# Moving the last two tiles' copies to SyncE, ScalarE's root and attention behind the gelu, and another cut between the last two sets

## The chip, the cores and the metric

One core of a Trainium2 chip runs the whole layer. The metric is the device time of that core in microseconds (us): the median of three runs was 2102.76 us (2102.34 to 2111.96). The execution that was profiled took 2104.69 us, of which the span of the trace is 2102.9 us.

The names of the engines in rows: PE is TensorE, DVE is VectorE, ACT is ScalarE, POOL is GpSimd, SP is SyncE. An engine name with a q behind it (SPq, ACTq, POOLq) is the part of the engine that issues DMAs and reads values into registers.

## The reference

6250 nodes with 256 values each, and 200,000 edges sorted by their destination. Cut to what matters:

```
xn  = layernorm(x)
gnn = relu(softmax-weighted sum over the edges of (xn @ W)[src] into dst, 4 heads, + bias)
mix = linear attention over all nodes (8 heads, kv = k^T v / N), then gelu(. @ w1 + b1) @ w2 + b2 + xn
x   = x + gnn + mix                                   # x1
z   = layernorm(layernorm(x)) * gamma + beta
logits = z @ Wr + br                                  # 8 experts, the best two of each node
y   = sum over the two of share_e * (gelu(z @ W1[e] + b1[e]) @ W2[e] + b2[e])
out = x1 + y
```

## The kernel before

The nodes lie in 49 tiles of 128 (tile 48 has 106). The kernel runs one long list of **steps** s = 0 to 210. Each engine walks through the same steps in its own order, written out in the code, and semaphores join them. There is no scheduler: what stands where is set by the tables that a planner at the top of the function fills (route_at, job_at, table_at, piece_at_step, final_at).

In steps 0 to 168 every step takes one group of 1024 edges (gather on GpSimd, products on VectorE, sums on TensorE). The sums come in from high destinations to low, so tiles 48 to 0 become complete one after the other. From step route_at[t] on tile t goes through its **route**: denominators (VectorE), attention = a division per head (ScalarE, L2209, one step later), sum and statistics (VectorE, L1833 to L1843), root (ScalarE, L2215, two steps later; this is the square root of the variance, and it and the gelu need different function tables), norm, transpose and logits (three later), choice of experts (four later), places (five later), sorting of the tile's rows by expert (six and seven later, L2503 on TensorE, L2245 on ScalarE), and then **hand-out**: the sorted tile goes to DRAM (keep_sorted, L1438), and eight copies, one for each expert, carry 128 rows each to that expert's region (L1452 on SyncE, L2236 on ScalarE). Each copy needs two numbers, where from and where to, that are read from memory into registers of the engine that issues it. Two copies make one piece (t, k), k = 0 to 3.

Every tile belongs to one of four **sets**: 48-24, 23-10, 9-5, 4-0. When a set is routed, a **table** on VectorE (L1921 and on) assigns its blocks of 128 rows to experts. From step 82 on each step also carries one **block** job. On TensorE this is the transposition of its input (turn_x, L2400), the second product of the block two steps older (L2466 and L2468, below called "down") and the first product of its own (L2428, "up"). ScalarE copies the turned input (L2166), copies the expert's weights (L2178, W_now) and applies the gelu (L2193). VectorE copies the result of the block three steps older out of PSUM (L1815, "the copy of the step"); a down of a step waits for the copy of the same step, since both use one bank, and a copy waits until the result before last has been stored. The stores go from SyncE (L1415) or, for blocks from step 169 on that are not in the last set, from ScalarE (L2249, four steps behind the block). The last block is at step 200.

From step 171 on, finished tiles are put together: x1 comes back from DRAM (SyncE, L1485, at final_at[t]), GpSimd gathers the two expert rows (L1599), VectorE adds (L1999 and L2002, "combine", at final_at[t] + 2), and SyncE writes the output (L1490). SyncE's own step is called c; in each c the block loads (L1402) come first, then keep_sorted, then the hand-out, then L1485 and L1490.

Steps 169 and on are called the tail. Tile 1 has route_at 169 and tile 0 has 170. Four tiles are **rushed** (RUSHED: 10, 5, 1, 0): SyncE makes pieces 0 and 1 at c = route_at + 9, and ScalarE pieces 2 and 3 at its step route_at + 10 (hand_out_rest). For tiles 1 and 0 these are c = 178 and 179 on SyncE, steps 179 and 180 on ScalarE.

Of the kernel before, what the change touches and what calls it, by code (L numbers as in the profile page):

```python
# [36 lines left out]
NEAR = 6  # L37
CUTS = (24, 10, 5)
CLOSED = (1, 2, 3)
# [16 lines left out]
def gps_layer(nc, x, xT, src_cols, dst_cols, W_turned, att_cols, inner_cols, src, dst, gnn_W, att_src, att_dst, gnn_bias, w_qkv, b_qkv, kln_g, kln_b, vln_g, vln_b,  # L56
# [5 lines left out]
    FULL = NT - 1  # L62
# [44 lines left out]
    NS = NG - COUNTED  # L107
# [12 lines left out]
    mix_at, route_at, table_at, final_at = {}, {}, [], {}  # L120
# [35 lines left out]
    HANDS = NE // BY_TWO  # L156
    RUSHED = tuple(t for t in SORTED if any(t == lo for _, lo in SETS[1:]) or route_at[max(t - 1, 0)] < route_at[t] + HANDS and t - 1 in (lo for _, lo in SETS[1:]))
    piece_at_step, waiting = {}, []
    for c in range(route_at[SORTED[0]] + 9, route_at[0] + 10):
        waiting += [(t, k) for t in SORTED if route_at[t] + 9 == c and t not in RUSHED for k in range(HANDS)]  # L160
        now = len(waiting) if any(route_at[t] + 9 == c for t in RUSHED) else 1 + c % 2 if len(waiting) > HANDS else 1
        piece_at_step[c] = waiting[:now] + [(t, k) for t in RUSHED if route_at[t] + 9 == c for k in range(HANDS // 2)]
        waiting = waiting[now:]
# [75 lines left out]
    with ExitStack() as ctx:  # L239
# [244 lines left out]
        def general_value(eng):  # L484
            return eng.value_load(general[0:1, 0:1], min_val=0, max_val=1)
# [608 lines left out]
        def loop_stage(ph):  # L1094
# [202 lines left out]
            def jobs_with(s):  # L1297
                return job_at[s] if s in job_at else None
# [853 lines left out]
            def on_scalar(act):  # L2152
# [137 lines left out]
                def part_weight(b):  # L2290
# [11 lines left out]
                    last.then_inc(part_ready, 1)  # L2302

                with act.If(general_value(act) == 0):
                    act.wait_ge(shifted_ready, 2)
# [7 lines left out]
                    for s in range(STEPS):  # L2313
                        for t in range(FULL, -1, -1):
                            if route_at[t] + 2 == s:
                                root(t)
                            if route_at[t] + 1 == s:
                                attention(t)
                        if 2 <= s < PAIRS + 2:
# [24 lines left out]
                        if jobs_with(s - 1):  # L2344
                            gelu(*jobs_with(s - 1))
                        for t in range(FULL, -1, -1):
                            if route_at[t] + 3 == s:
                                take_tile(t)
# [6 lines left out]
                        for t in RUSHED:  # L2355
                            if route_at[t] + 10 == s:
                                for k in range(HANDS // 2, HANDS):
                                    hand_out_rest(t, k)
# [1414 lines left out]
```

## Time and profile before

| | us |
|---|---|
| median of 3 runs | 2102.76 |
| profiled execution | 2104.69 |
| its span | 2102.9 |
| TensorE busy | 1761.4 (84%) |
| VectorE busy | 1595.5 (76%) |
| GpSimd busy | 1455.5 (69%) |
| ScalarE busy | 1213.1 (58%) |

These shares are means over parts that differ. Between 1700 and 1850 us TensorE has no idle time; in the tail, which begins at 1889 us, no engine is busy all the time. A row's idle time in brackets tells how long the engine stood still ahead of that instruction and what ended this. To find a step in the tail, count the ups back from the last: the up of step 200 starts at 2071.01, and each step has one.

### The profile page before, as it was taken

To read this page: it belongs to the slowest core of one execution; us is meant where nothing else is said; L and a number is where in the kernel's file an instruction comes from. 1 tells how busy PE (TensorE), PEld (TensorE's weight loads), DVE (VectorE), ACT (ScalarE), POOL (GpSimd) and SP (SyncE) were. 2 spreads that over 40 slices of the span, in tenths; PEclk is the share of its full clock that TensorE was granted. 3 is DMA by queue.
4 is the path that set the end of the run, shared out by engine and by line. 5 is a ranking of instruction groups with operands and counts; after the bars stand their busy time and mean duration, and the time that the engine had idled before them with its cause. 6 is when DMAs were issued, how large, how long until landed. Compare 5 with 4: busy or idle time off the path is not lost. (4 is left out here: it accounts for less than half of the span.)

```text
span 2102.9 us, 40583 instructions
## 1 busy us (share of the span) xinstructions
PE 1761.4 (84%) x10047; PEld 1429.2 (68%) x10048; DVE 1595.5 (76%) x3938; ACT 1213.1 (58%) x2310; POOL 1455.5 (69%) x1586
## 2 busy tenths in 40 slices
PE   8499999678677777767888898988998999998795
PEld 6367777556565556545767777766887888886584
DVE  7678888567677777779888888978986898884343
ACT  4433333235455555434877787867875798965452
POOL 3277777777777777777766777775777777763463
PEclk9799999888787878777999999998999999999898
DMA  9676665686666666666677777786678777856683
GB/s 334 153 192 173 174 172 157 195 276 182 174 179 184 176 181 180 172 166 163 188 199 200 216 213 212 210 248 174 188 202 243 203 214 206 216 151 204 193 253 115
DMA packets 289176, 411.77 MB, mean 196 GB/s; under 512 B 108856, under 2 KB 211520, under 8 KB 285227
## 3 DMA queue, kind: packets, MB, share of 16 engines
q0 software_dynamic: 74208, 206.08, 36.5%
q1 hardware_dynamic: 196968, 187.45, 30.2%
q10 hardware_dynamic: 17762, 15.56, 2.7%
q8 instruction: 90, 1.47, 0.3%
q14 instruction: 148, 1.20, 0.2%
HBM read 354.61 MB, written 90.98 MB: 212 GB/s over the span
## 5 line engine op out<-in xcount | busy, mean ns | idle before, releaser
L1577 POOL DMA_INDIRECT rows_g<-node_table,src_all x1347 | 1283.4, 953 | 474.9 <-issue 408.1
L2388 PE MATMUL psB<-rows_g,pick_e 128*128 128x260 f32 x2704 | 747.6, 438 | 143.4 <-issue 120.8
L2388 PEld LDWEIGHTS psB<-rows_g,pick_e 128*128 128x128 f32 x2704 | 582.8, 221 | 267.0 <-issue 161.3
L1752 DVE TENSOR_TENSOR rows_g<-rows_g,psD 128x2048 f32<-128x2048 f32 x169 | 384.7, 2276 | 0.0
L2160 ACT ACTIVATE pick_n<-local_row 128x1024 bf16<-128x1024 bf16 x169 | 178.6, 1057 | 173.7 <-PE psA L2377 165.2
L2428 PEld LDWEIGHTS psC<-xnT,W_now 128*128 128x128 f32 x1904 | 232.5, 193 | 11.3 <-ACT W_now L2178 5.0
L2428 PE MATMUL psC<-xnT,W_now 128*128 128x128 f32 x1904 | 234.4, 277 | 2.0 <-ACT W_now L2178 1.8
L1723 DVE TENSOR_TENSOR pick_e<-psD,slot_all 128x1024 f32<-128x1024 f32 x169 | 203.4, 1204 | 0.1
L2156 ACT ACTIVATE local_row<-local_row,minus_id 128x1024 bf16<-128x1024 bf16 x169 | 191.6, 1134 | 15.9 <-DVE both_f L2062 8.7
L1599 POOL DMA_INDIRECT rows_g<-set_dram,places x98 | 95.2, 972 | 112.2 <-issue 62.3
L1815 DVE COPY xn<-psD 128x256 f32<-128x256 f32 x119 | 50.1, 421 | 155.8 <-PE psD L2484 53.1
L2377 PE MATMUL psA<-window,pick_n 128*128 128x24 bf16 x1352 | 59.5, 174 | 102.2 <-DVE psD L1733 55.8
L2377 PEld LDWEIGHTS psA<-window,pick_n 128*128 128x128 bf16 x1352 | 54.9, 99 | 125.1 <-issue 124.1
L1741 DVE TENSOR_TENSOR p_both_e<-rows_g,psD 128x64 f32<-128x64 f32 x169 | 48.6, 288 | 114.8 <-DMA rows_g<-node_table,src_all 108.5
L2178 ACT ACTIVATE W_now<-W_f 128x1024 f32 x119 | 125.2, 1052 | 18.0 <-issue 16.7
L2468 PE MATMUL psD<-W_f,hidT_more 128*128 x480 | 124.2, 403 | 0.0
L2222 ACT ACTIVATE xdT<-psA 128x256 f32<-128x256 f32 (+1 forms) x49 | 18.8, 385 | 178.2 <-PE psA L2477 178.2
L2468 PE MATMUL psD<-W_f,hidT 128*128 x472 | 119.4, 397 | 0.0
L2468 PEld LDWEIGHTS psD<-W_f,hidT_more 128*128 128x128 f32 x480 | 89.1, 196 | 17.8 <-issue 0.7
L2166 ACT ACTIVATE xnT<-psA 128x256 f32<-128x256 f32 x119 | 44.3, 373 | 98.6 <-PE psA L2400 83.5
L2468 PEld LDWEIGHTS psD<-W_f,hidT 128*128 128x128 f32 x472 | 85.9, 192 | 16.7 <-issue 0.2
L2516 PE MATMUL psC<-W_f,xnT 128*128 128x512 f32 (+1 forms) x196 | 89.9, 602 | 2.5 <-DMA xnT<-in_xT_dram 2.5
(389 smaller groups left out, 2920.2 us busy)
## 6 DMA issues: line engine op xcount, KB each, us to landing
local_row<-local_dram SPq DMA_DIRECT2D x169, 256.0 KB, 4.1
sent_dram<-sorted_dram SPq DMA_DIRECT2D x176, 128.0 KB
rows_g<-node_table,src_all POOLq DMA_INDIRECT x1347
set_dram<-xn SPq DMA_DIRECT2D x104, 128.0 KB
xnT<-in_xT_dram SPq DMA_DIRECT2D x96, 128.0 KB
xin<-sent_dram SPq DMA_DIRECT2D x90, 128.0 KB
sent_dram<-zero_dram SPq DMA_DIRECT2D x24, 384.0 KB
acc<-node_table SPq DMA_DIRECT2D x49, 128.0 KB
```

What stands on the lines that cost most here:

```text
L1577: pool.indirect_dma_start(out=rows_g[:, r, j], out_offset=None, in_=node_table, in_offset=bass.IndirectOffsetOnAxis(ap=src_all[:, g, j:j + ...
L1599: pool.indirect_dma_start(out=final_home(f)[0][0:rows, c], out_offset=None, in_=set_dram[span_of[x]], in_offset=bass.IndirectOffsetOnAxis( ...
L1723: dve.tensor_tensor(pick_e[:, r], ids_here.unsqueeze(1).broadcast_to([P, EG, P]), slot_all[:, g].unsqueeze(2).broadcast_to([P, EG, P]), AL ...
L1752: dve.tensor_tensor(heads, heads, p_here.unsqueeze(3).broadcast_to([P, EG, HEADS, C]), ALU.mult).then_inc(ph_ready, 1)
L2156: act.activation(local_row[:, r], local_row[:, r], ACT.Abs, bias=minus_id[:]).then_inc(away_ready, 1)
L2160: act.activation(pick_n[:], local_row[:, r], ACT.Relu, bias=1.0, scale=-1.0).then_inc(pick_n_ready, 1)
L2178: act.activation(W1_now[:].rearrange("p k n -> p (k n)"), W1_f[:, bass.ds(experts[n], 1)].rearrange("p e k n -> p (e k n)"), ACT.Copy).the ...
L2377: last = pe.matmul(ps_pick[:, j * 6 * HEADS:(j + 1) * 6 * HEADS], pick_n[:, j * P:(j + 1) * P], window[:, w].rearrange("p k a -> p (k a)") ...
L2388: last = pe.matmul(ps_sum[s % 2][:, 0:AW], pick_e[:, s % SLOTS, j], rows_g[:, s % RING, j, 0:AW], start=(j == 0), stop=(j == EG - 1))
L2428: last = pe.matmul(inner_bank(n)[:, c * P:(c + 1) * P], W1_now[:, k, c * P:(c + 1) * P], xnT[:, u, k], start=(k == 0), stop=(k == KT - 1))
L2468: last = pe.matmul(ps_small[:, down_at], turned_rows(n, kind)[:, c], W2_f[:, bass.ds(e, 1), c], start=False, stop=(c == HK - 1))
L2516: last = pe.matmul((ps_up, ps_hT)[u][0:rows, :], xnT[:, u, k, 0:rows], wkv_s[:, k], start=(k == 0), stop=(k == KT - 1))
```

## The change

Three edits. CUTS moves the last cut from 5 to 3, so the last two sets are tiles 9-3 (21 blocks) and 2-0 (13 blocks), where they were 9-5 and 4-0 with 17 each. The sum of the blocks and the step of each job stay; the blocks of steps 184 to 187 now belong to the third set. The third set's table moves from step 142 to 156, the filling with zeros before its last tiles (eight DMAs of 384 KB) from c = 137 to c = 149, and the rushed tile of that set is 3 instead of 5. The last cut's table stays at step 176. Three tiles instead of five are put together behind the last block.

For tiles routed at step 169 or later (tiles 1 and 0) SyncE makes all four pieces and ScalarE none. And in steps after 169 ScalarE's root and attention stand behind the gelu, where they stood first in the step.

```
-CUTS = (24, 10, 5)
+CUTS = (24, 10, 3)
...
-        piece_at_step[c] = waiting[:now] + [(t, k) for t in RUSHED if route_at[t] + 9 == c for k in range(HANDS // 2)]
+        piece_at_step[c] = waiting[:now] + [(t, k) for t in RUSHED if route_at[t] + 9 == c for k in range(HANDS if route_at[t] >= NS else HANDS // 2)]
...
+                def roots_and_attention(s):
+                    for t in range(FULL, -1, -1):
+                        if route_at[t] + 2 == s:
+                            root(t)
+                        if route_at[t] + 1 == s:
+                            attention(t)
...
-                        for t in range(FULL, -1, -1):
-                            if route_at[t] + 2 == s:
-                                root(t)
-                            if route_at[t] + 1 == s:
-                                attention(t)
+                        if s <= NS:
+                            roots_and_attention(s)
...
                         if jobs_with(s - 1):
                             gelu(*jobs_with(s - 1))
+                        if s > NS:
+                            roots_and_attention(s)
...
-                            if route_at[t] + 10 == s:
+                            if route_at[t] + 10 == s and route_at[t] < NS:
                                 for k in range(HANDS // 2, HANDS):
                                     hand_out_rest(t, k)
```

HANDS is 4 and NS is 169.

SyncE at c = 178, as a piece of the difference (rows with + are new). L1384 and L1402 are the load of a block, L1438 stores the sorted tile 0, L1449 and L1450 read the numbers of one piece, and L1452 issues a copy:

```order
+L1384 TENSOR_LOAD acc
+L1384 ISA x2
+L1402 ISA
+L1402 DMA pick_e<-sent_dram 128x256
 L1438 DMA sorted_dram<-weff 128x2x256
+L1449 TENSOR_LOAD cuts
+L1449 ISA x4
+L1450 TENSOR_LOAD cuts
+L1450 ISA x4
+L1452 ISA
+L1452 DMA sent_dram<-sorted_dram 16x2048
```

From here tile 1's pieces stand four times in a row instead of twice, then the outputs (L1490) and the x1 loads (L1485) of c = 178, then tile 0's four pieces instead of two, then those of c = 179. The block loads of c = 177 to 180 come one by one; before, all four stood at c = 180.

ScalarE at step 179, a piece of the difference. L2234 and L2235 read the two numbers of a copy:

```order
 L2193 ACTIVATE hidT_more<-psC,acc 128x128
-L2234 TENSOR_LOAD cuts
-L2234 ISA x2
-L2235 TENSOR_LOAD cuts
-L2235 ISA x2
-L2236 ISA
-L2236 DMA sent_dram<-sorted_dram 16x2048
```

The six rows with - stand four times in step 179 and four times in step 180, and all are gone; the store L2249 follows the gelu at once.

ScalarE from the end of step 172 to the gelu of step 173, before. L2222 takes tile 1's transposed rows:

```order
L2193 ACTIVATE hidT<-psC,acc 128x128
L2222 ACTIVATE xdT<-psA 128x256
L2166 ACTIVATE xnT<-psA 128x256
L2176 TENSOR_LOAD blk_expert
L2176 ISA x2
L2178 ISA
L2178 ACTIVATE W_now<-W_f 128x1024
L2193 ISA
L2193 ACTIVATE hidT_more<-psC,acc 128x128
```

And the same stretch now, from tile 0's root on:

```order
L2215 ACT_TABLE_LOAD
L2215 ACTIVATE std_r<-mv_r,eps_sq 128x1
L2222 ACTIVATE xdT<-psA 128x256
L2166 ACTIVATE xnT<-psA 128x256
L2176 TENSOR_LOAD blk_expert
L2176 ISA x2
L2178 ISA
L2178 ACTIVATE W_now<-W_f 128x1024
L2193 ISA
L2193 ACT_TABLE_LOAD
L2193 ACTIVATE hidT_more<-psC,acc 128x128
```

Tile 0's root stood ahead of step 172's gelu and now stands behind it, so L2222 comes after the root, and the gelu of step 173 now loads its table again, where before it was the gelu of step 172 that did. The number of table loads is the same.

## Rows read from the trace of the kernel before

**Rows 1.** Busy time by stretch: start:end, length, busy of each engine, clock, DMA.
```profile
1965.00:1990.00 25.00, 13.23 (x76) 11.18 (x75) 4.89 (x14) 5.74 (x15) 7.68 (x9) 0.80 0.60 182
```

**Rows 2.** Waits of TensorE, 1903 to 2075 us: total, times, longest.
```profile
PE psD L2466 <- DVE xn L1815: 15.6, 8, 8.6
```

**Rows 3.** Timeline of SyncE's queue: start, length, operation, count.
```profile
1957.12 0.39 SPq L1438 DMA_DIRECT2D sorted_dram<-weff  x1
1960.13 5.23 SPq L1452 DMA_DIRECT2D sent_dram<-sorted_dram  x4
1966.58 0.55 SPq L1485 DMA_DIRECT2D rows_g<-x_dram  x1
1969.89 5.60 SPq L1452 DMA_DIRECT2D sent_dram<-sorted_dram  x4
...
1974.11 1.38 SPq L1452 DMA_DIRECT2D sent_dram<-sorted_dram  x2
...
1976.23 0.87 SPq L1485 DMA_DIRECT2D rows_g<-x_dram  x2
1984.85 3.75 SPq L1402 DMA_DIRECT2D pick_e<-sent_dram  x4
...
1989.67 0.39 SPq L1485 DMA_DIRECT2D rows_g<-x_dram  x1
```

**Rows 4.** Timeline of ScalarE, in the tail.
```profile
1903.36 1.07 ACT L2209 ACTIVATE acc<-acc,rden_f 128x64 f32<-128x64 f32 x4
...
1906.50 1.12 ACT L2193 ACTIVATE hidT<-psC,acc 128x128 f32<-128x128 f32 x4
...
1922.17 0.36 ACTq L2249 DMA_DIRECT2D set_dram<-xn  x1
...
1954.39 1.28 ACT L2193 ACT_TABLE_LOAD   x1
...
1955.78 0.33 ACTq L2249 DMA_DIRECT2D set_dram<-xn  x1
...
1965.64 7.10 ACTq L2236 DMA_DIRECT2D sent_dram<-sorted_dram  x4
```

**Rows 5.** Timeline of VectorE, in the tail.
```profile
1904.46 0.43 DVE L1833 TENSOR_TENSOR psD<-acc,gnn_bias_b 128x256 f32<-128x256 f32 x1 [1.15 <-ACT acc L2209]
...
1907.03 0.42 DVE L1815 COPY xn<-psD 128x256 f32<-128x256 f32 x1 [0.28 <-PE psD L2468]
...
1926.44 0.42 DVE L1815 COPY xn<-psD 128x256 f32<-128x256 f32 x1 [0.18 <-DMA set_dram<-xn]
...
1987.54 0.42 DVE L1815 COPY xn<-psD 128x256 f32<-128x256 f32 x1 [0.56 <-PE psD L2468]
...
1993.03 0.48 DVE L1999 SCALAR_TENSOR_TENSOR rows_g<-rows_g,share 128x256 f32<-128x256 f32 x1 [3.94 <-DMA rows_g<-x_dram]
...
2084.96 0.48 DVE L1999 SCALAR_TENSOR_TENSOR rows_g<-rows_g,share,acc 128x256 f32<-128x256 f32 x1 [6.59 <-DMA rows_g<-set_dram,places]
...
2094.97 0.49 DVE L1999 SCALAR_TENSOR_TENSOR rows_g<-rows_g,share,acc 128x256 f32<-128x256 f32 x1 [1.52 <-DMA rows_g<-set_dram,places]
```

**Rows 6.** Timeline of TensorE, in the tail; the first row is from step 147.
```profile
1690.42 2.05 PE L2428 MATMUL psC<-xnT,W_now 128*128 128x128 f32 x16 [1.26 <-ACT W_now L2178]
...
1909.13 1.99 PE L2468 MATMUL psD<-W_f,hidT 128*128 x8
...
1975.77 0.39 PE L2466 MATMUL psD<-acc 24*128 24x256 bf16 x1 [8.64 <-DVE xn L1815]
1976.09 3.78 PE L2468 MATMUL psD<-W_f,hidT_more 128*128 x8
...
1991.54 2.05 PE L2428 MATMUL psC<-xnT,W_now 128*128 128x128 f32 x16
...
2015.92 1.95 PE L2428 MATMUL psC<-xnT,W_now 128*128 128x128 f32 x16
...
2067.09 1.95 PE L2428 MATMUL psC<-xnT,W_now 128*128 128x128 f32 x16
```

## The prediction

> **What bounds the kernel now.** I read the engine shares first, then busy time by stretch, then the waits of TensorE in the tail, and last the timelines of the five engines there. Through the last part of the edge steps TensorE never stands still. The tail is different: in 1965 to 1990 us TensorE works 13.23 of 25 us at a mean granted clock of 0.80, VectorE 4.89, ScalarE 5.74 [rows 1]. Nobody is the bottleneck there, so an order or a queue is. In the tail TensorE waits 15.6 us for VectorE's copy (the down of a step needs the copy of the step), 8.6 of it in one piece [rows 2]. That piece ends at 1975.77, step 180 [rows 6]: ScalarE was issuing four hand-out copies for 7.10 us [rows 4], its store stood behind them, and VectorE's copy waited for that store. This is the stall that the change takes away.
>
> Two more facts of the tail matter. First, SyncE issues slowly: four copies take 5.23 us from the first to the last (tile 1) and 5.60 us (tile 0) [rows 3]. The two copies of a piece take 1.38, so reading the numbers between two pieces costs 5.23 - 2*1.38 = 2.5 to 5.60 - 2*1.38 = 2.8 us. A piece is 3.9 to 4.2 us of SyncE's time. Second, VectorE's combines wait for x1 loads that SyncE issues in the same list: the load of c = 180 was issued at 1989.67 [rows 3], and VectorE stood 3.94 us until it landed, at 1993.03 [rows 5], step 182. x1 loads of c serve VectorE's step c + 2. So before the change SyncE was already, for one step, what the tail waited for.
>
> **Part 1, the copies.** All times here are those of the profiled execution, before any shift by part 2. The sorted tile 0 is stored at 1957.12, and the first copy follows at 1960.13, behind the reading of its numbers [rows 3]. Four pieces instead of two for tile 1 add 2*3.9 = 7.8 us. The x1 load of c = 178 moves from 1966.58 to 1974.4 and its end to 1975.0. A block load now stands ahead of tile 0's pieces; four of them took 3.75 us from first to last with three number reads between, so one with its read is some 1.15 us. Tile 0's four pieces start at 1975.0 + 1.15 + 2.8 = 1978.9 and end 3*4.1 + 1.4 later, at 1992.6; before, they ended at 1969.89 + 5.60 = 1975.5. So the two x1 loads of c = 179 go from 1976.23 to about 1993.4 and end at 1994.2. Landing takes 3.4 us (1993.03 against 1989.67), so they are there at 1997.4, and VectorE needs 1 us for the last combine. Its copy of step 182, at 1987.54 before [rows 5], comes at 1998.4 at the earliest, and with it step 182's down.
>
> On the other side, what does the removal give? The copy of step 180 needs only ScalarE's store, which is issued some 7 us earlier. TensorE goes through step 181's up by about 1982 to 1984 and then stands until 1998.8: 15 us of new idle time. The 8.64 us of ScalarE's stall and the smaller one after it do go, but what is late next is SyncE's x1 load, 17 us later than it was, and it decides. After such an idle time the first down is slow: 3.78 us at 1976.09, after 8.64 us idle, against 1.99 at 1909.13 [rows 6]; with the up behind it I take 2.1 us. So step 182's up starts at 1998.8 + 0.3 + 3.6 = 2002.7 (1991.54 before), and ends 11.3 us later than before. This is the first term: **+11.3**. Its bounds: with pieces of 3.4 us instead of 3.9 to 4.1 (2.0 us for the reads), four more pieces are 13.6 instead of 16 us, and with no slow down the term is 11.3 - 2.4 - 2.1 = 6.8; with pieces of 4.4 and a landing of 5 us it is 14.5.
>
> A rule of the Trainium skill speaks for the change here: in DMA: Bandwidth & Descriptors, under "Issuing engines are not separate DMA queues", it says that issuing on several engines at once only saves the sequencers' issue time, "which is usually small relative to the DMA itself". By that rule the move costs SyncE nothing that counts. The rows say that here it is not small, since each copy is preceded by its reads (3.9 us a piece). [...]
>
> **Part 2, root and attention behind the gelu.** Tile 1's attention (step 170) comes behind the gelu that ends at 1906.50 + 1.12 = 1907.62 and so ends at 1908.7; VectorE waited for it until 1904.46 [rows 4, 5]. VectorE is in order: first sum, statistics and tile 0's denominators move by 4.3 us, and the copy of step 171 behind them goes from 1907.03 to 1911.4. The down of that step, at 1909.13, follows to about 1911.8: 2.7 us. The same happens with tile 0, and one thing more: the gelu of step 173 gets a table load that it did not have. A store on ScalarE's queue behind such a load goes out only when it is done, 1.39 us behind the load's start (1954.39, 1955.78), where without it the store at 1922.17 went out right behind the weights' copy [rows 4]. By my count that store goes to about 1926, since the turned inputs come 2 us later and the load adds 1.8. VectorE's copy at 1926.44 waits for just this store [rows 5]. Second term: **+3.8**. Bounds: -1 (the weights' copies and the gelu now come 0.6 us earlier, and this is all that counts) to +5. What follows is one chain up to the sorted tile 0 at 1957.12, so the term adds to the first. The gelu's side gains nothing, since TensorE waits for VectorE's copies and not for the gelu.
>
> The page ScalarE: Activation LUTs ("What ACT_TABLE_LOAD costs") gives 1.28 us for the load and 1.38 us of drain for every switch. The load's 1.28 is in the rows. The four switches stay four; a drain would make the term 1.4 larger.
>
> **Part 3, the last cut.** The blocks of steps 184 to 187 no longer hang on tiles 1 and 0. TensorE did not wait for their loads before, so this gains nothing by itself; it only makes it harmless that the last copy of tile 0 is issued at 1992 instead of 1982. But their stores change from SyncE to ScalarE, which issues them a step later. With ScalarE's stores, ups 182 to 187 took (2015.92 - 1991.54)/5 = 4.88 us a step; with SyncE's, ups 187 to 199 took (2067.09 - 2015.92)/12 = 4.26 [rows 6]. Four steps change sides: 4*0.62 = **+2.5** (0 to 3).
>
> At the end three tiles are gathered and combined instead of five. The first combines came at 2084.96 and 2094.97 for tiles one and five, 2.50 us apart [rows 5]: **-5.0** (-4.5 to -5.5), all on the path that ends the kernel. The combines of tiles 4 and 3 stand in the steps before, where VectorE is more than half idle.
>
> **Part 4, in the edge steps.** The third set's table, its zero filling and ScalarE's rushed copies move by 12 to 14 steps. The rushed copies of tile 5 cost TensorE 1.26 us, at step 147 [rows 6]; those of tile 3 will cost about as much. The table and the filling come into steps where TensorE has no slack and leave steps where it has some: I take **0**, with -3 and +3 as bounds.
>
> **Sum.** 11.3 + 3.8 + 2.5 - 5.0 + 0 = +12.6 on the profiled execution's 2104.69: 2117.3. The median of the runs is 1.93 lower, so 2115.4; I say 2115.
>
> **Rivals.**
> (a) The copies' issue is hidden, as the skill's rule would have it. Then steps 179 to 183 run at 4.88 us each; step 183's up, 5.0 behind that of 182, was at 1996.5, and step 179's, just ahead of the four copies, at about 1965.0, so 31.5 becomes 19.5: -12. With -5.0, +2.5 and part 2 at 0 to 3.8 this is -14.5 to -10.7, a median of 2088 to 2092: faster. For it speaks that ScalarE's two stalls are real; against it the x1 load behind the last copy, which has no way around. 12%.
> (b) The same mechanism as in my forecast, but part 2 is about 0 and the reads are at their cheap end: 8.9 + 0 + 2 - 5 = +6, a median of 2105 to 2111, no measurable change. For it: part 2 hangs on a chain that I count. 25%.
> (c) The change does nothing to the pace because the set boundary was what held the tail (the first load of the last set at 1984.85 waits for the last copy). The new boundary then gives four blocks of slack and the end is 5 us earlier, with part 1 gone: about 2100. I see no wait of TensorE for that load; 5%.
> (d) As my forecast, with the upper bounds of parts 1, 2 and 4, or a clock that stays low for longer after 15 us idle: +18 and more, above 2120. 13%.
> My forecast proper, 2111 to 2120, has 45%.
>
> **Chances.** A measurement of this kernel tells 0.5% (10.5 us) from no change. Slower by more: three quarters of the forecast (above 2113.3) and (d), 0.34 + 0.13, with a little of (b), 0.50. Faster by more: 0.12 of (a). The rest, 0.38, is within. The range is 2100 to 2123: it leaves out (a) and the far end of (d).
>
> **What would show it.** Right: no hand-out row of ScalarE after 1950; sixteen copies in SyncE's queue over some 33 us; VectorE's longest tail wait is at a combine, for x1, 10 us or more; TensorE's longest idle time is in step 182 and above 12 us, ended by VectorE's copy, with a slow down behind it; the store of step 173 later by 2 to 4 us against the end of the last sums; three combines at the end. Wrong: no idle time over 5 us in steps 181 to 183 (then the copies cost less than their rows say), or tile 0's sorted store at the same distance from the last sums (then part 2 is nothing), or edge steps that end at another time than 1889 by more than 3 us.

## The result and the profile after

| | before | after |
|---|---|---|
| median, us (lowest to highest, 7 runs each) | 2103.78 (2100.78 to 2111.96) | 2121.88 (2117.59 to 2123.41) |
| profiled execution | 2104.69 | 2123.41 |
| its span | 2102.9 | 2121.6 |

The ratio is 1.0075 (95% interval 1.0059 to 1.0091): slower by 0.75%, which is more than the 0.5% that a measurement tells from no change.

Five marks cut the tail into pieces that can be compared one by one: the ups of steps 169, 182, 187 and 200, and the store of the sorted tile 0 on SyncE. The lines above L2301 kept their numbers, those of TensorE's block work moved by 6 (L2428 is now L2434, L2466 is L2472, L2468 is L2474).

| piece of the span, us | before | after | difference | predicted |
|---|---|---|---|---|
| start to up of step 169 | 1902.7 | 1907.6 | +4.9 | 0 (-3 to 3) |
| to the store of sorted tile 0 | 54.4 | 58.5 | +4.1 | +3.8 |
| to up 182 | 34.4 | 44.5 | +10.1 | +11.3 |
| to up 187 | 24.4 | 26.1 | +1.7 | +2.5, up to 200 |
| to up 200 | 55.1 | 57.8 | +2.7 | in the line above |
| to the end | 31.9 | 27.0 | -4.9 | -5.0 |
| sum | 2102.9 | 2121.6 | +18.7 | +12.6 |

SyncE's queue after (start, length, line, operation, count) answers to [rows 3]:

```profile
1966.16 0.39 SPq L1438 DMA_DIRECT2D sorted_dram<-weff  x1
1969.11 13.45 SPq L1452 DMA_DIRECT2D sent_dram<-sorted_dram  x8
...
1983.81 0.42 SPq L1485 DMA_DIRECT2D rows_g<-x_dram  x1
...
1987.98 12.92 SPq L1452 DMA_DIRECT2D sent_dram<-sorted_dram  x8
...
2001.65 0.85 SPq L1485 DMA_DIRECT2D rows_g<-x_dram  x2
```

Sixteen copies stand between 1969.11 and 2000.90, with the one x1 load of c = 178 between the two groups of eight, and the two of c = 179 behind the second. The waits of VectorE and TensorE in 1885 to 2122 us (engine, line waited with, releaser: total, times, longest) answer to [rows 2]:

```profile
DVE rows_g L1999 <- DMA rows_g<-x_dram: 28.1, 3, 16.5
...
PE psD L2472 <- DVE xn L1815: 31.1, 11, 12.0
```

Before, the combines waited 7.2 us in all for x1. VectorE's timeline after, for [rows 5]; the number in brackets is the idle time ahead of a row:

```profile
1913.64 0.43 DVE L1833 TENSOR_TENSOR psD<-acc,gnn_bias_b 128x256 f32<-128x256 f32 x1 [5.40 <-ACT acc L2209]
...
1935.12 0.43 DVE L1815 COPY xn<-psD 128x256 f32<-128x256 f32 x1 [2.47 <-DMA set_dram<-xn]
...
1986.70 0.48 DVE L1999 SCALAR_TENSOR_TENSOR rows_g<-rows_g,share 128x256 f32<-128x256 f32 x1 [10.23 <-DMA rows_g<-x_dram]
...
2004.49 0.49 DVE L1999 SCALAR_TENSOR_TENSOR rows_g<-rows_g,share 128x256 f32<-128x256 f32 x1 [16.45 <-DMA rows_g<-x_dram]
...
2006.34 0.42 DVE L1815 COPY xn<-psD 128x256 f32<-128x256 f32 x1
...
2108.59 0.48 DVE L1999 SCALAR_TENSOR_TENSOR rows_g<-rows_g,share,acc 128x256 f32<-128x256 f32 x1 [5.70 <-DMA rows_g<-set_dram,places]
...
2113.58 0.48 DVE L1999 SCALAR_TENSOR_TENSOR rows_g<-rows_g,share,acc 128x256 f32<-128x256 f32 x1 [1.51 <-DMA rows_g<-set_dram,places]
```

And TensorE's, for [rows 6]:

```profile
1916.25 0.28 PE L2472 MATMUL psD<-acc 24*128 24x256 bf16 x1 [2.29 <-DVE xn L1815]
...
1988.19 0.39 PE L2472 MATMUL psD<-acc 24*128 24x256 bf16 x1 [7.37 <-DVE xn L1815]
1988.51 3.78 PE L2474 MATMUL psD<-W_f,hidT 128*128 x8
...
2006.91 0.39 PE L2472 MATMUL psD<-acc 24*128 24x256 bf16 x1 [11.97 <-DVE xn L1815]
2007.22 3.63 PE L2474 MATMUL psD<-W_f,hidT_more 128*128 x8
2010.69 1.95 PE L2434 MATMUL psC<-xnT,W_now 128*128 128x128 f32 x16
...
2094.62 1.95 PE L2434 MATMUL psC<-xnT,W_now 128*128 128x128 f32 x16
```

Read together: each group of eight copies holds up one x1 load, each late load holds up one combine, and behind each combine stands the copy that the down waits for. So 8.64 us of idle time [rows 6] became 7.37 + 11.97. The combines at the end are three: 2108.59 to 2113.58 is two times 2.50 us, where [rows 5] has four times.

Busy time by stretch (length, busy of TensorE, weight load, VectorE, ScalarE, GpSimd, granted clock, DMA share, GB/s) shows the hole beside the stretch of [rows 1], which is now the better one:

```profile
1983.00:2008.00 25.00, 7.83 (x30) 6.36 (x31) 4.37 (x13) 3.07 (x9) 3.18 (x4) 0.57 0.43 128
...
1965.00:1990.00 25.00, 16.40 (x105) 14.05 (x104) 5.92 (x15) 11.03 (x29) 8.92 (x11) 0.87 0.53 156
```

### The profile page after: what moved, and what is told of

Its sections match the earlier page's. It is cut to its first block and busy times, and to the rows that moved or that the text cites. A ratio compares the mean times of both kernels' runs of the same rounds, so it can differ in the third digit from the quotient of the medians.

```text
span 2121.6 us, 40575 instructions
## 1 busy us (share of the span) xinstructions
PE 1770.1 (83%) x10047; PEld 1437.4 (68%) x10048; DVE 1597.1 (75%) x3938; ACT 1213.6 (57%) x2310; POOL 1455.2 (69%) x1586
## 5 line engine op out<-in xcount | busy, mean ns | idle before, releaser
L1752 DVE TENSOR_TENSOR rows_g<-rows_g,psD 128x2048 f32<-128x2048 f32 x169 | 384.8, 2277 | 0.0
L2434 PEld LDWEIGHTS psC<-xnT,W_now 128*128 128x128 f32 x1904 | 234.8, 194 | 10.9 <-ACT W_now L2178 4.1
L2434 PE MATMUL psC<-xnT,W_now 128*128 128x128 f32 x1904 | 235.5, 277 | 2.7 <-ACT W_now L2178 2.6
L2383 PEld LDWEIGHTS psA<-window,pick_n 128*128 128x128 bf16 x1352 | 54.4, 99 | 115.8 <-issue 111.1
L2474 PE MATMUL psD<-W_f,hidT_more 128*128 x480 | 125.8, 407 | 0.0
L2474 PE MATMUL psD<-W_f,hidT 128*128 x472 | 122.5, 404 | 0.0
L2222 ACT ACTIVATE xdT<-psA 128x256 f32<-128x256 f32 (+1 forms) x49 | 18.9, 385 | 166.1 <-PE psA L2483 166.1
L2166 ACT ACTIVATE xnT<-psA 128x256 f32<-128x256 f32 x119 | 44.5, 374 | 115.4 <-PE psA L2406 115.4
L2474 PEld LDWEIGHTS psD<-W_f,hidT_more 128*128 128x128 f32 x480 | 90.1, 198 | 18.1 <-issue 0.4
L2474 PEld LDWEIGHTS psD<-W_f,hidT 128*128 128x128 f32 x472 | 87.9, 196 | 17.6 <-issue 0.4
```

The lines of the kernel that those rows point to most:

```text
L1752: dve.tensor_tensor(heads, heads, p_here.unsqueeze(3).broadcast_to([P, EG, HEADS, C]), ALU.mult).then_inc(ph_ready, 1)
L2383: last = pe.matmul(ps_pick[:, j * 6 * HEADS:(j + 1) * 6 * HEADS], pick_n[:, j * P:(j + 1) * P], window[:, w].rearrange("p k a -> p (k a)") ...
L2434: last = pe.matmul(inner_bank(n)[:, c * P:(c + 1) * P], W1_now[:, k, c * P:(c + 1) * P], xnT[:, u, k], start=(k == 0), stop=(k == KT - 1))
L2474: last = pe.matmul(ps_small[:, down_at], turned_rows(n, kind)[:, c], W2_f[:, bass.ds(e, 1), c], start=False, stop=(c == HK - 1))
```

## The experiments

Each was timed against the kernel before on the same chip. "Tail" is the distance from the up of step 169 to the end of the span, 200.2 us before and 214.0 after. It is the better measure of a change to the tail, because the start of step 169's up differs between profiled executions of like edge steps by some us. The columns behind the median are three of the pieces of the table above, and "tail", each from the one profiled execution of the run. The medians of different rows stem from different chips and rounds, in which the kernel before had medians of 2103.78 to 2107.54 us, so rows are compared by their ratios.

| run | ratio (95%) | median, us | to up 169 | to sorted tile 0 | to up 182 | tail |
|---|---|---|---|---|---|---|
| before | 1 | 2103.78 | 1902.7 | 54.4 | 34.4 | 200.2 |
| after | 1.0075 (1.0059 to 1.0091) | 2121.88 | 1907.6 | 58.5 | 44.5 | 214.0 |
| e1_roots_first | 1.0059 (1.0037 to 1.0080) | 2117.27 | 1904.0 | 56.9 | 44.0 | 211.2 |
| e2_scalar_copies | 1.0046 (1.0029 to 1.0063) | 2116.05 | 1913.1 | 56.5 | 38.7 | 204.5 |
| e3_cut_alone | 1.0028 (1.0014 to 1.0042) | 2110.97 | 1900.1 | 55.8 | 37.9 | 203.5 |
| e4_copies_alone | 1.0037 (1.0022 to 1.0051) | 2113.34 | 1902.8 | 56.3 | 43.7 | 212.7 |
| e5_roots_alone | 1.0010 (0.9999 to 1.0021) | 2107.12 | 1901.7 | 55.0 | 34.8 | 202.6 |
| e6_scalar_x1 | 0.9978 (0.9966 to 0.9989) | 2100.42 | 1904.2 | 60.0 | 22.3 | 197.1 |
| e7_first_x1 | 0.9965 (0.9953 to 0.9978) | 2097.01 | 1905.6 | 56.6 | 22.1 | 189.5 |
| e8_first_x1_cut5 | 1.0013 (1.0002 to 1.0024) | 2107.15 | 1903.3 | 57.1 | 23.0 | 208.1 |
| e9_sync_stores | 0.9945 (0.9932 to 0.9957) | 2094.36 | 1907.5 | 56.5 | 23.6 | 187.2 |
| e10_store_first | 1.0002 (0.9991 to 1.0014) | 2105.42 | 1899.0 | 57.9 | 33.8 | 204.7 |
| e11_unrushed | 0.9938 (0.9920 to 0.9955) | 2089.58 | 1900.4 | 56.5 | 22.6 | 185.9 |
| e12_cut_unrushed | 1.0001 (0.9990 to 1.0013) | 2107.42 | 1904.1 | 56.9 | 37.3 | 205.6 |

The three edits alone, and after without the order or the copies, come first. After without the cut was not run; the pair e7 and e8 asks for the cut in another setting.

**e1: after, but root and attention first in every step.**

```
-                        if s <= NS:
-                            roots_and_attention(s)
+                        roots_and_attention(s)
...
-                        if s > NS:
-                            roots_and_attention(s)
```

> The changed kernel, with ScalarE's root and attention first in every step again. Theory (root and attention behind the gelu cost 3.8 to 4.1 us on the chain to tile 0's sorted store): the time falls by about 4 us against the changed kernel, to 0.6% over the kernel before; tile 0's sorted store comes 54 to 55 us behind the up of step 169 (58.5 in the changed kernel, 54.4 before); no table load in the gelu of step 173. Rival (the order costs nothing, the shift is chance): no more than 1 us, store 58 us behind. The stall of VectorE at x1 in steps 180 and 181 stays in both.

The ratio falls from 1.0075 to 1.0059 and the tail by 2.8 us, but the two intervals overlap. The store of the sorted tile 0 came 56.9 us behind up 169 and not the 54 to 55 expected, so only 1.6 of the 4.1 us went with the order.

**e2: after, but ScalarE makes pieces 2 and 3 of tiles 1 and 0 again.**

```
-... for k in range(HANDS if route_at[t] >= NS else HANDS // 2)]
+... for k in range(HANDS // 2)]
...
-                            if route_at[t] + 10 == s and route_at[t] < NS:
+                            if route_at[t] + 10 == s:
```

> The changed kernel, with pieces 2 and 3 of tiles 1 and 0 on ScalarE again. Theory (SyncE's sixteen copies hold back the x1 loads, which costs 10 to 11 us up to step 182): VectorE's waits of 10.2 and 16.5 us for x1 go, TensorE's 8.6 us behind ScalarE's store in step 180 comes back, and the time is 9 to 11 us under the changed kernel, 0.2 to 0.4% over the kernel before. Rival (taking the copies off ScalarE is worth its 8.6 + 3.1 us of stalls and something else slowed the tail): the time rises by up to 12 us over the changed kernel.

Up 182 comes 5.8 us earlier and the tail is 9.5 us shorter; x1 is no longer among VectorE's four longest waits, and the old stall is back. ScalarE first, then TensorE:

```profile
1981.38 6.35 ACTq L2236 DMA_DIRECT2D sent_dram<-sorted_dram  x4
1987.78 0.59 ACTq L2249 DMA_DIRECT2D set_dram<-xn  x1
```
```profile
1991.12 0.39 PE L2472 MATMUL psD<-acc 24*128 24x256 bf16 x1 [8.85 <-DVE xn L1815]
```

The store goes out 0.05 us behind the last of the four copies, and TensorE stood for 8.85 us until VectorE's copy, which waits for that store, was done. The tail fell by what was expected; the ratio fell by 0.29% (some 6 us), which is less than the 9 to 11 us expected.

**e3: before, with only the cut.** `CUTS = (24, 10, 3)`.

> The kernel before with the cuts at 24, 10, 3 alone. Theory: 5.0 us less at the end (three tiles instead of five), 2.5 to 4.5 us more between steps 182 and 200 for stores on ScalarE, so -2.5 to -0.5 us from there; in the edge steps either 0 (the 4.9 us by which the changed kernel's up of step 169 was late are chance) or +5 (they come from the table and the zero filling that stand 14 and 12 steps later): in all 0.999 to 1.002 of the kernel before. Rival (the boundary of the sets held the tail): 5 us or more faster.

Slower by 0.28% and not faster, as a change that takes 5 us from the end should have been, and outside the 0.999 to 1.002 expected. The profiled execution, at 2105.61 us, is the fastest of twelve, so its pieces show less than the medians do. The end did get 5.0 us shorter (26.9). The tail as a whole grew by 3.3 us all the same: 3.5 us more between the sorted tile 0 and up 182, and 2.8 more in ups 187 to 191, whose copies wait for stores that ScalarE now issues. VectorE's waits for stores were 40.7 us in all before, the longest 10.6, and are now

```profile
DVE xn L1815 <- DMA set_dram<-xn: 64.2, 13, 11.9
```

What it costs in the edge steps is taken up below, with e12.

**e4: before, with only the copies.** The two edits of the change on RUSHED, without the rest.

> The kernel before with all copies of tiles 1 and 0 on SyncE alone; cuts and ScalarE's order as before. Theory: VectorE waits 10 us and more for x1 in steps 180 and 181, as in the changed kernel, and since four block loads (3.75 us) stand ahead of the x1 load of c = 180, also in step 182; the time rises by 11 to 16 us, 0.5 to 0.8%. Rival (ScalarE's stall was the thing, and only the other edits are harmful): 8 to 12 us faster than the kernel before.

The ratio rose by 0.37% and not by the 0.5 to 0.8% expected, while the tail grew by 12.5 us, as expected. Up 182 comes 9.3 us later against the sorted tile 0, with the two idle times of after and nothing else of the change:

```profile
1981.12 0.39 PE L2469 MATMUL psD<-acc 24*128 24x256 bf16 x1 [6.51 <-DVE xn L1815]
...
1998.86 0.39 PE L2469 MATMUL psD<-acc 24*128 24x256 bf16 x1 [10.52 <-DVE xn L1815]
```

**e5: before, with only ScalarE's new order.** The new function and its two calls, without the rest.

> The kernel before with ScalarE's root and attention behind the gelu in the tail, and nothing else. Theory: VectorE waits some 5 us for tile 1's attention, the copies of steps 171 to 174 come later, and tile 0's sorted store stands 58 to 59 us behind the up of step 169 instead of 54.4; the tail (up of step 169 to the end of the span) grows from 200.2 to 204 us, the time by 0.1 to 0.25%. Rival (the order costs nothing by itself; the changed kernel's 4 us were scatter of the tail, as the 1.4 to 1.9 us of kernels with the old order are): tail of 200 to 201 us.

The interval holds no change. VectorE waits for tile 1's attention as it does in after, and yet the store of sorted tile 0 comes only 0.6 us later:

```profile
1907.57 0.43 DVE L1833 TENSOR_TENSOR psD<-acc,gnn_bias_b 128x256 f32<-128x256 f32 x1 [5.29 <-ACT acc L2209]
```

Steps 171 and 173 took 6.7 and 8.2 us, against 4.6 and 5.5 before, but step 172 5.6 against 6.8 and step 176 8.0 against 9.7, so part of the time was made up inside the chain. What the order costs stays open, and it is small beside the scatter of this piece. In the ten profiled executions with the old order the piece took 54.4 to 57.9 us, mean 56.5, and the kernel before is the shortest of them. In the four with the new order (after, e2, e5, e6) it took 55.0 to 60.0, mean 57.5. The closest pair, e7 against e6, gives 3.4 us.

The three alone add up to 0.37 + 0.10 + 0.28 = 0.75%, which is the whole, though each of the three is known only to 0.11 to 0.15% either way. The next runs ask whether the x1 load behind the copies is what makes SyncE's copies dear.

**e6: after, with ScalarE issuing the x1 loads and the output stores of steps 178 to 184.** SyncE's list then holds the block loads, the store of the sorted tile 0 and the copies there. ScalarE does them at the end of its step, behind its store.

```
+LENT = range(178, 185)
...
-                            if final_at[t] == c and t >= KEPT_FROM:
+                            if final_at[t] == c and t >= KEPT_FROM and c not in LENT:
...
+                        for t in final_at:
+                            if final_at[t] == s and t >= KEPT_FROM and s in LENT:
+                                x1_again(act, t)
+                            if sum_at[t] + 1 == s and s in LENT:
+                                give(act, t)
```

> The changed kernel, but in steps 178 to 184 ScalarE issues the x1 loads and the output stores, which stand behind SyncE's sixteen copies in the changed kernel. The copies all stay on SyncE. Theory (the copies cost time only because the x1 loads stand behind them): VectorE's waits of 10.2 and 16.5 us for x1 go, up of step 182 comes 24 to 28 us behind the sorted tile 0 (44.5 in the changed kernel, 34.4 before), the tail shrinks from 214 to 194 to 198 us and the time falls under that of the kernel before by up to 0.3%. Rival (the sixteen copies hold the tail by themselves, through the DMA queue or through the first load of the last set, which waits for them): the tail stays above 208 us, and a wait for a block's rows or a set_dram store takes the place of the x1 wait.

With the same sixteen copies on the same queue, the stretch to up 182 is 22.3 us long instead of 44.5, and the waits are

```profile
DVE rows_g L2000 <- DMA rows_g<-x_dram: 3.7, 2, 2.4
...
PE psD L2478 <- DVE xn L1816: 14.4, 11, 3.1
```

The median is 21.5 us below that of after (0.97% by the ratios, some 20 us), and the ratio is below 1. This is the run that shows the cause: the copies are not dear by themselves but by what stands behind them. The output stores moved together with the x1 loads, and no run parts the two; the wait that shrank, from 28.1 us to 3.7, is the one for x1.

**e7: the same, with root and attention first,** by the edit of e1.

> As the kernel with ScalarE's x1 loads in steps 178 to 184, and with root and attention first in the step again. Theory: another 3 to 4 us less in front of tile 0's sorted store (the edit of the order costs what it costs whatever stands behind it): tail of 190 to 195 us, time 0.2 to 0.5% under the kernel before. Rival: same as the kernel with the order behind the gelu.

0.9965 against 0.9978, with intervals that overlap; the sorted tile 0 comes 3.4 us sooner behind up 169, and ups 187 to 191 are 3.2 us shorter, where the order of the roots no longer matters. So the 3.4 us between the medians need not all be the order's.

**e8: e7 with the old cut.** `CUTS = (24, 10, 5)`.

> All copies of tiles 1 and 0 on SyncE, x1 loads and output stores of steps 178 to 184 on ScalarE, root and attention first, and the cuts at 24, 10, 5 as in the kernel before. Theory: with the old cut the first block of the last set is needed at step 184, and its load waits for the sixteenth copy, 34 us behind the sorted tile 0; TensorE is there some 27 us behind it, so a wait of 6 to 10 us for a block's rows appears at step 183 or 184, and the end takes 32 us instead of 27: the time is 7 to 14 us over the same kernel with the new cut, 0.0 to 0.3% over the kernel before. Rival (the cut costs in the edge steps and by ScalarE's stores as much as it gives): the same time as with the new cut, 2097 us on this chip's scale.

Slower by 0.48% than e7 with the new cut, and more than I expected. The first block of the last set now waits for the sixteenth copy:

```profile
1999.63 0.69 PE L2409 MATMUL psA<-ident,pick_e 128*128 128x128 f32 x2 [14.24 <-DMA pick_e<-sent_dram]
```

So the cut costs 0.28% on the kernel before and gives 0.48% once the tail no longer waits for x1. It is worth nothing by itself, but with all copies on SyncE and x1 out of their way it is needed.

**e9: e7, with the blocks of steps 184 to 187 stored by SyncE.** Before the change they were in the last set, which SyncE stores.

```
+SYNC_AGAIN = 184
...
-... c - 3 < LATE or job[2] == len(SETS) - 1):
+... c - 3 < LATE or c - 3 >= SYNC_AGAIN):
...
-                        if s - 4 >= LATE and jobs_with(s - 4) and jobs_with(s - 4)[2] < len(SETS) - 1:
+                        if LATE <= s - 4 < SYNC_AGAIN and jobs_with(s - 4):
```

> As the kernel with ScalarE's x1 loads and root and attention first, and the blocks of steps 184 to 187 stored by SyncE at their step plus 3, as before the change of the cut. Theory (the new cut costs 2.5 to 4.5 us because these four stores went to ScalarE): ups 187 to 191 take 17 to 18 us instead of 18 to 20, time 2 to 3 us less, 0.3 to 0.6% under the kernel before: the fastest of all. Rival (SyncE is late there too): no gain.

Ups 182 to 191 took 42.3 us instead of 46.8. The ratio went from 0.9965 to 0.9945, and the two intervals just overlap. The copies take SyncE about as long as in e7 (15.15 and 14.00 us for eight), and TensorE hardly waits for VectorE's copy, 7.5 us in all where it was 8.5 in e7:

```profile
1967.01 15.12 SPq L1468 DMA_DIRECT2D sent_dram<-sorted_dram  x8
...
1986.45 13.85 SPq L1468 DMA_DIRECT2D sent_dram<-sorted_dram  x8
```
```profile
PE psD L2476 <- DVE xn L1817: 7.5, 9, 1.1
...
PE psA L2410 <- DMA pick_e<-sent_dram: 0.7, 1, 0.7
```

**e10: before, with ScalarE's store ahead of its rushed copies.** It asks what the stall was worth that the change set out to remove.

```
-                        for t in RUSHED:
-                            if route_at[t] + 10 == s:
-                                for k in range(HANDS // 2, HANDS):
-                                    hand_out_rest(t, k)
...
+                        for t in RUSHED:
+                            if route_at[t] + 10 == s:
+                                for k in range(HANDS // 2, HANDS):
+                                    hand_out_rest(t, k)
```

> The kernel before, with ScalarE's block store ahead of its rushed copies in steps 179 and 180, where it stood behind them. Theory (the 8.6 us are the store's delay, and behind the store the weights' copy of the next step is delayed just as long): the copy of step 180 no longer waits, but TensorE's up of step 180 waits for the weights instead, so that 2 to 4 us are gained, time 0.1 to 0.2% less. Rival (the store was all of it): up of step 180 comes 5 us behind that of 179 instead of 14.7, and the time falls by 8 to 11 us.

1.0002: nothing. VectorE's copy is no longer late (5.9 us of waits instead of 16.2 in the tail), but the next step's weights and turned input stand behind the four copies too, so steps 180 to 182 still took 10.3, 9.7 and 5.9 us (14.7, 7.7 and 4.2 before):

```profile
PE psC L2428 <- ACT W_now L2178: 9.0, 4, 4.6
...
PE psD L2466 <- DVE xn L1815: 5.9, 5, 1.7
```

**e11: e9, with tile 3 not rushed.** SyncE makes its four pieces one in each c from 159 to 162, and ScalarE none at step 160.

```
-    RUSHED = tuple(t for t in SORTED if any(t == lo for _, lo in SETS[1:]) or ...
+    RUSHED = tuple(t for t in SORTED if any(t == lo for _, lo in SETS[1:]) and t != CUTS[-1] or ...
```

> As the fastest kernel so far (all copies on SyncE, x1 on ScalarE for steps 178 to 184, root first, new cut, late stores on SyncE), with tile 3's pieces handed out by SyncE one a step at c = 159 to 162 instead of two at once on SyncE and two on ScalarE at step 160. Theory (a rushed tile's copies on ScalarE cost TensorE 1.3 us in the edge steps, as those of tile 5 did): 1 to 2 us less in front of the up of step 169, nothing in the tail. Rival: no difference that can be measured, or the first load of the third set waits.

The fastest version by median, 2089.58 us; its ratio of 0.9938 (0.9920 to 0.9955) is not told apart from e9's 0.9945. Steps 160 to 164, by the starts of VectorE's L1752, took 42.2 us instead of 46.2 in e9, twice to four times the 1 to 2 us expected. Its tail in the stretch of [rows 1] has TensorE busy for most of the time, at a full granted clock:

```profile
1965.00:1990.00 25.00, 21.94 (x147) 19.26 (x147) 9.31 (x24) 12.51 (x31) 15.55 (x17) 1.00 0.85 258
```

**e12: e3, with tile 3 not rushed,** by the edit of e11.

> The kernel before with the cuts at 24, 10, 3, and tile 3's four pieces handed out by SyncE one a step (c = 159 to 162) instead of half of them on ScalarE at step 160. Theory (with the new cut the stretch from step 148 to the up of step 169 takes 220 us instead of 211 to 213, and ScalarE's four copies at step 160 are 4 us of that, the table and the zero filling the rest): that stretch takes 216 us, and the time is 3 to 5 us less than with the cut alone (1.0028 of the kernel before), so 1.0005 to 1.0015. Rival (the copies are hidden, as those of tile 5 were but for 1.3 us): the stretch stays at 220 us and the ratio at 1.002 to 1.003.

1.0001 against e3's 1.0028. Steps 160 to 164 fell from 46.1 to 42.2 us here too, so by the ratios the rushed copies of tile 3 are 0.27% of the cut's price, nearly all of it; the traces show 3.9 us, which is 0.19%.

## The cut in the edge steps

Where did the 4.9 us ahead of step 169 come from? Between step 142 and up 169 before and after, cut at the starts of steps 148, 156, 160 and 164 (same columns as above; first before, then after):

```profile
1625.50:1690.00 64.50, 61.10 (x395) 53.14 (x394) 57.73 (x168) 51.48 (x110) 48.95 (x52) 0.95 0.79 211
1690.00:1770.30 80.30, 79.88 (x557) 71.19 (x558) 69.72 (x183) 73.30 (x170) 61.13 (x63) 1.00 0.80 213
...
1807.50:1848.90 41.40, 41.40 (x289) 36.97 (x288) 34.81 (x89) 38.18 (x85) 31.34 (x34) 1.00 0.81 214
1848.90:1902.70 53.80, 51.85 (x333) 45.01 (x332) 36.41 (x89) 26.61 (x58) 28.29 (x29) 0.97 0.48 132
```
```profile
1624.90:1686.90 62.00, 59.63 (x399) 52.32 (x398) 52.87 (x141) 52.36 (x118) 47.37 (x48) 0.97 0.79 207
1686.90:1771.50 84.60, 79.90 (x533) 70.22 (x534) 68.81 (x179) 67.40 (x154) 64.48 (x67) 0.96 0.85 237
...
1810.20:1856.80 46.60, 43.96 (x288) 38.60 (x287) 36.06 (x93) 38.38 (x89) 35.39 (x37) 0.96 0.77 204
1856.80:1907.60 50.80, 50.80 (x339) 44.73 (x338) 36.56 (x89) 27.65 (x61) 22.44 (x24) 1.00 0.44 121
```

TensorE was busy for 271.4 us of the 277.2 before and 271.5 of the 282.7 after: the same work, and 5.5 us more idle time. The cut does this by itself: the same distance is 281.5 us in e3, and it is 279.8 in e12 and 277.8 in e11. It isn't chance either: the five profiled executions with the old cut took 275.0 to 279.4 us for it, the seven with the new cut and tile 3 rushed 281.5 to 285.3. After, two pieces of it stand out. Tile 3's four copies at step 160 hold up the weights (as tile 5's did at step 147, [rows 6], for 1.26 us), and the filling with zeros at c = 149 holds up the gathers:

```profile
1723.76 1.64 PE L2394 MATMUL psB<-rows_g,pick_e 128*128 128x260 f32 x3 [4.33 <-issue]
...
1835.55 2.95 PE L2434 MATMUL psC<-xnT,W_now 128*128 128x128 f32 x16 [2.64 <-ACT W_now L2178]
```
```profile
1705.09 7.38 SPq L1476 DMA_DIRECT2D sent_dram<-zero_dram  x8
```
```profile
1720.76 0.22 DVE L1741 TENSOR_TENSOR p_both_e<-rows_g,psD 128x64 f32<-128x64 f32 x1 [6.59 <-DMA rows_g<-node_table,src_all]
```

Before, the same eight DMAs at 1581.63 made VectorE wait too, 7.33 us at 1598.00, but steps 136 to 142 took 60.8 us against 60.7 without them in after. TensorE was idle for 7.65 us of the 65 between 1560 and 1625 with the filling and for 7.37 without it. Before, it was idle for 0.42 us of 80.3 where the filling stands now. The same shows in every trace: steps 148 to 156 took 80.4 us in the five with the old cut and 83.8 to 87.1 in the nine with the new one, where VectorE waits 5.4 to 7.9 us for a gather some 15 us behind the first DMA of the filling. For tile 3's copies e11 and e12 show the price (they also spread SyncE's two pieces over more steps). That the filling costs the 4.3 us is read from the traces: no run moves it by itself.

## Why the prediction was right or wrong

The side was right (slower by more than 0.5%, given 0.50) and 2121.88 lies in the range, but above the 2111 to 2120 of the forecast proper. The parts add up to +18.7 where +12.6 was forecast, so that the range held it by 1.1 us is partly luck. It is in the band of rival (d), and of the upper bounds named there only that of part 4 is met (and passed): part 1 was below its forecast and part 2 near it.

**Part 1, copies: right.** +11.3 forecast (its own numbers give 2002.7 - 1991.54 = 11.2), +10.1 in after and +9.3 in e4. The copies are 16 in 1969.11 to 2000.90, 31.8 us (some 33 forecast). A piece took the 3.9 to 4.1 us forecast: eight copies hold four pairs and three reads between them, so a piece is (13.45 - 1.38)/3 = 4.0 us for tile 1 and (12.92 - 1.38)/3 = 3.8 for tile 0. From the store of the sorted tile 0 to VectorE's copy of step 182 it was 40.2 us, 1.1 less than forecast: 0.8 less up to the x1 loads of c = 179, 0.3 less from there to the copy. I placed all of the idle time in step 182, above 12 us. It came in two pieces: 7.37 in step 181 and 11.97 in 182. I had worked out that the x1 load of c = 178 would be 7.8 us later and then drew no wait from it.

**Part 2, root and attention: the size was met (+4.1 against +3.8), but largely by luck.** The kernel before is the shortest of ten executions with the old order, whose mean lies 2.1 us above it, so half of the 4.1 is scatter; e5 measured +0.6. The attention's wait is where it was forecast (5.40 us in after), the gelu's table load has moved, and a store goes out behind it. ScalarE after, for [rows 4]:

```profile
1911.54 1.12 ACT L2193 ACTIVATE hidT<-psC,acc 128x128 f32<-128x128 f32 x4
1912.54 1.07 ACT L2209 ACTIVATE acc<-acc,rden_f 128x64 f32<-128x64 f32 x4
...
1928.14 1.06 ACT L2178 ACTIVATE W_now<-W_f 128x1024 f32 x1 [0.26 <-issue]
1929.22 1.28 ACT L2193 ACT_TABLE_LOAD   x1
1930.61 0.36 ACTq L2249 DMA_DIRECT2D set_dram<-xn  x1
```

The two local delays are real, but e5 shows that the chain behind them can take most of it back. I added 2.7 us and more to the chain as if nothing in steps 172 to 180 had slack.

**Part 3, the cut.** The end is right (-5.0, measured -4.9, -5.0 in e3). The stores were sized +2.5 at most 3 and came to +4.4 over ups 182 to 200. e9 supports the cause: with SyncE's stores ups 182 to 191 are 4.5 us shorter.

**Part 4, the edge steps: the step that failed.** I took 0 with +3 as the bound and measured +4.9. The text had the reason in it ("steps where TensorE has no slack") and then let the two sides cancel. The copies of tile 5 were priced at the 1.26 us of idle time in [rows 6], and those of tile 3 taken as the same; when tile 3 is not rushed, steps 160 to 164 are 3.9 to 4.0 us shorter. The filling was not priced at all, and steps 148 to 156 took 4.3 us more. The sign that I had named for this part could not show it: the last edge step's L1752 starts at 1891.5 instead of 1888.8 us, 2.7 later and inside the 3 us I allowed.

**Rival (a)** is out: by the rule of the Trainium skill that I set against the rows (DMA: Bandwidth & Descriptors, "Issuing engines are not separate DMA queues"), the issue time would have been small, and eight copies held SyncE for 12.92 to 15.44 us. e6 shows the rival's gain as well: 22.3 us to up 182 where the kernel before took 34.4, once the loads behind the copies have another queue. That is about the 12 us which the rival forecast. **Rival (b)** needed the reads at their cheap end (3.4 us a piece) and part 2 at about 0. The first is wrong, since a piece took 3.8 to 4.0 us; the second is open. Its sum of +6 was passed by parts 1, 3 and 4. **Rival (c)** is wrong for the kernel before and turns right later: e8 waits 14.24 us at the old boundary. It was a bound that stood behind another.

**What the prediction did not ask:** what else stands behind ScalarE's copies. It named the store. e10 takes the store out from behind them, adds nothing to SyncE, and the time is the same, for the turned input and the weights' copy of the next step stand behind them too. Before, ScalarE's first work of step 180 shows it:

```profile
1973.48 0.38 ACT L2166 ACTIVATE xnT<-psA 128x256 f32<-128x256 f32 x1 [8.06 <-DMA sent_dram<-sorted_dram]
```

Only with the copies off ScalarE altogether did the stall go: steps 180 and 181 took 5.7 and 4.1 us in e6, against 14.7 and 7.7 before. So that edit could give some 12 us (34.4 against 22.3 us to up 182, in which the small x1 wait of before goes too), and with the x1 loads behind the copies on SyncE it lost 10 instead.

## What to carry to other kernels

When work moves to another in-order queue, write down what stands behind it there and what each of those waits for; price the move by the most urgent of them, not by the work. The same list is due for the queue that the work leaves: what stood behind it there is what the move can give back. A load that the next step needs belongs on a queue that holds nothing slow, and here that was worth some 20 us (e6 against after, output stores included). Work that is moved into a stretch where the bounding engine has no slack must be priced anew there: the same eight DMAs went with no loss that shows in steps 136 to 142, and steps 148 to 156 took 4.3 us more with them.

## What was not expected of the hardware

- A copy whose addresses are read from memory costs its queue some 2 us, whichever engine issues it: in after 3.8 to 4.0 us for a piece of two on SyncE. From the first copy to the end of the last, eight on SyncE took 12.92 to 15.44 us and four on ScalarE 6.3 to 7.1 us, and this leaves out the reading ahead of the first.
- Eight DMAs of 384 KB, issued in 7.38 us, were followed by a gather that came 6.59 us late for VectorE, and the DMA share of the 84.6 us around them was 0.85, against 0.80 without them. That the one made the other late is inferred from the nine traces that have both there.
- The granted clock was 0.57 in the 25 us with the two idle times, near the lower of its two levels (1.2 GHz), and 1.00 in 1965 to 1990 us of e11, where TensorE was busy for 21.94 us. Downs behind the idle times took 3.78 and 3.63 us, against 1.99 at 1909.13 [rows 6].
- The table load at 1929.22 started 0.02 us behind the end of the weights' copy. The Trainium skill (ScalarE: Activation LUTs, "What ACT_TABLE_LOAD costs") speaks of a drain of 1.38 us at a switch; here the traces show none. Each of the six loads in the tail of after starts 0.02 us behind the end of the activation ahead of it, and the next activation starts 0.01 us behind the load. The load's 1.28 us agree. The store behind the load at 1929.22 went out 1.39 us after its start.
